# Graph network on one Trainium2 core: one-hots of the second sweep on ScalarE, direction terms of the second tile scaled there and added on VectorE

## The reference, cut to what matters

```
edge_dst, edge_src = src, dst              # of the graph
p0, p1 = pre-layer of x                    # p1: 128 channels x 3 directions
ip1 = sum over m of p1[edge_dst] * p1[edge_src] / 3
w = ssp(edge_attr @ W_f1) @ W_f2 * (ssp([p0, p0, ip1] @ W_s1) @ W_s2)
w1, w2, w3, w4 = split(w, 4)               # 128 each
x0e, x1e = gate-layer of x, at edge_src
out0 = w1 * x0e * sh0 + w4 * (sum over m of x1e[m] * sh1[m]) / sqrt(3)
out1[m] = w2 * x0e * sh1[m] + w3 * x1e[m] * sh0      # m = 1..3
out = segment_sum([out0, out1], edge_dst)
```

## Time and profile before

| | |
|---|---|
| median of 3 runs | 1173.89 us (1171.5 to 1177.24) |
| profiled execution | 1171.3 us, its span 1169.6 us |
| PE busy in the span | 907.8 us (78%) |
| DVE busy | 833.4 us (71%) |
| POOL busy | 731.0 us (63%) |
| ACT busy | 511.1 us (44%) |
| L1135, sums with the one-hot, PE | 184.1 us, x1328 |
| L1137, sums with the scaled one-hots, PE | 134.7 us, x332 |
| L1197, scaled rows, ACT | 161.5 us, x498 |
| L1103, L1106, L1108, dot products, POOL | 122.2, 60.4 and 60.5 us, x83 each |

### The profile page before, as it was taken

One profiled execution on the slowest core, in us unless ns is written; L12 is line 12 of the kernel. 1 busy time (PEld: TensorE's weight loads), 2 busy tenths in 40 slices (PEclk: granted clock), 3 DMA queues, 4 the chain that ended last, 5 costly groups with the idle time before them and its releaser, 6 DMA issues. The chain is left out here.

```text
span 1169.6 us, 23040 instructions
## 1 busy us (share of the span) xinstructions
PE 907.8 (78%) x5587; PEld 623.7 (53%) x5588; DVE 833.4 (71%) x2120; ACT 511.1 (44%) x1484; POOL 731.0 (63%) x768
## 2 busy tenths in 40 slices
PE   1315644449999997675699999999999999999973
PEld 1203322225555553564476777776777776777753
DVE  8441001137777776673599999999999999999967
ACT  1113211012323232463466666666666666666630
POOL 2777777757777773010677777777777777777610
PEclk9998766869999999898799999999999999999997
DMA  9300101157878785012655555555555555555402
GB/s 346 87 15 25 34 24 33 52 162 240 243 240 239 238 240 118 30 65 84 205 171 175 176 168 170 177 165 167 182 164 169 173 171 169 178 164 170 146 4 90
DMA packets 107466, 171.54 MB, mean 147 GB/s; under 512 B 36038, under 2 KB 79162, under 8 KB 107292
## 3 DMA queue, kind: packets, MB, share of 16 engines
q0 software_dynamic: 31584, 122.92, 33.5%
q1 hardware_dynamic: 72060, 46.71, 13.1%
q10 hardware_dynamic: 3776, 1.38, 0.5%
HBM read 151.61 MB, written 19.35 MB: 146 GB/s over the span
## 5 line engine op out<-in xcount | busy, mean ns | idle before, releaser
L749 PE MATMUL ps<-ring,aw 128*128 128x512 f32 x332 | 185.8, 648 | 23.0 <-DVE aw L697 14.3
L1093 POOL DMA_INDIRECT ring<-tab_d,ed x166 | 160.5, 967 | 66.3 <-issue 31.6
L408 POOL DMA_INDIRECT slots_d<-stage,stage_pos x157 | 153.3, 977 | 71.4 <-issue 48.7
L666 POOL DMA_INDIRECT ring<-xt_d,ed x166 | 158.8, 957 | 58.4 <-issue 43.0
L1103 POOL TENSOR_TENSOR dot<-ring,ed 128x768 f32<-128x768 f32 x83 | 122.2, 1472 | 108.7 <-issue 88.3
L1135 PE MATMUL ps<-oh,mm_sb 128*128 128x128 f32 x1328 | 184.1, 282 | 4.9 <-DVE acc L1276 4.9
L1135 PEld LDWEIGHTS ps<-oh,mm_sb 128*128 128x128 f32 x1328 | 161.1, 192 | 23.3 <-issue 17.7
L1197 ACT ACTIVATE ohs<-oh,ed 128x128 f32<-128x128 f32 x498 | 161.5, 389 | 0.0
L1228 ACT ACTIVATE S_sb<-ps 128x512 f32<-128x512 f32 x166 | 90.1, 595 | 115.3 <-PE ps L1184 115.3
L1137 PE MATMUL ps<-ohs,mm_sb 128*128 128x384 f32 x332 | 134.7, 488 | 0.0
L1251 DVE TENSOR_TENSOR ps<-S_sb,ps 128x1024 f32<-128x1024 f32 x83 | 102.0, 1229 | 19.1 <-ACT S_sb L1228 18.3
(11 more groups left out here) (210 smaller groups left out, 1799.9 us busy)
## 6 DMA issues: line engine op xcount, KB each, us to landing
ilb<-f_d SPq DMA_DIRECT2D x83, 128.0 KB
ed<-slots_d SPq DMA_DIRECT2D x166, 38.0 KB, 3.5
tab_d<-tabrow SPq DMA_DIRECT2D x5, 896.0 KB, 3.7
f_d<-ft SPq DMA_DIRECT2D x83, 38.0 KB
slots_d<-fill SPq DMA_DIRECT2D x7, 418.0 KB, 4.4
ring<-xt_d,ed POOLq DMA_INDIRECT x166, 4.0
hcat<-f_d SPq DMA_DIRECT2D x83, 32.0 KB
s0b<-f_d SPq DMA_DIRECT2D x83, 32.0 KB
```

The source lines that it names most:

```text
L408: g.indirect_dma_start(slots_d[:, :], bass.IndirectOffsetOnAxis(ap=stage_pos[:, h, k:k + 1], axis=0), stage[:, h, k, :], None).then_inc(sc ...
L666: gp.indirect_dma_start(xg[:, c, k, :], None, xt_d[:, :], bass.IndirectOffsetOnAxis(ap=ed[:, c, k, JD:JD + 1].bitcast(I32), axis=0))\
L749: pe.matmul(ps[:, 2 * u, :], aw[:, r, k, :], xg[:, c, k, 0:D], start=(alone or k == 0), stop=(alone or k == 1))
L1093: gp.indirect_dma_start(xj[:, r, k, :], None, tab_d[:, :], bass.IndirectOffsetOnAxis(ap=ed[:, c, k, JD:JD + 1].bitcast(I32), axis=0))\
```

## The change

- The one-hots of the second sweep are made on ACT instead of DVE: `away` = |node - row number| by two Abs, then Relu(1 - away) over both tiles. They stand between `inner_out` and the scaled rows.
- `scaled_rows` are made for the group's first tile alone: three instead of six.
- For the second tile ACT scales `w2 * x0e` by each `sh1` into `scaled` (three instructions, behind `log_part`), and DVE adds these to the out1 part of the tile's messages (`add_scaled`, between `accumulate` and `products`). `sums(1)` on PE then needs only the four matmuls with the plain one-hot, and waits for `scaled_added`.
- On POOL `gather` stands ahead of `dots`, and `dots` of group g waits for the turned one-hot of group g+2, which DVE makes in the same round, instead of the one-hot of g-1.
- On ACT `node_part` moves to the end of the round.
- The counters `issue1` and `issue2` become the common `issue`.

```diff
@@ pool
                     gp.wait_ge(xj_in[c], n * 32)
-                    after(gp, oh_ready, g)
+                    gp.wait_ge(ohT_ready, min(g + 3, NG) if isinstance(g, int) else g + 3)
                     after(gp, msg_ready, g - 1)
...
-                pipelined(gp, (2, dots), (0, gather), ring=U)
+                pipelined(gp, (0, gather), (2, dots), ring=U)
@@ tensor, sums(k)
+                        if k == 1:
+                            pe.wait_ge(scaled_added, g + 1)
                         for m in range(4):
-                            pe.matmul(psA[:, P * m:P * m + P], mm_sb[:, u, k, P * m:P * m + P], oh[:, u, k, :],
-                                      start=((alone or k == 0) and m == 0), stop=False)
-                        mm = pe.matmul(psA[:, P:D], mm_sb[:, u, k, D:D + P], ohs[:, u, k, :, :].rearrange("p m n -> p (m n)"),
-                                       start=False, stop=(alone or k == 1))
+                            mm = pe.matmul(psA[:, P * m:P * m + P], mm_sb[:, u, k, P * m:P * m + P], oh[:, u, k, :],
+                                           start=((alone or k == 0) and m == 0), stop=(k == 1 and m == 3))
+                        if k == 0:
+                            mm = pe.matmul(psA[:, P:D], mm_sb[:, u, k, D:D + P], ohs[:, u, :, :].rearrange("p m n -> p (m n)"),
+                                           start=False, stop=alone)
@@ scalar
+                def one_hot(g, c, n):
+                    u = c % 2
+                    act.wait_ge(ed2[c], n * 64)
+                    after(act, sum_ready, upto(g - 2))
+                    for k in range(2):
+                        ins = act.activation(away[:, k, :], iota[:, :], ACT.Abs, scale=-1.0, bias=ed[:, c, k, IL:IL + 1])
+                    ins.then_inc(away_ready, 1)
+                    act.wait_ge(away_ready, g + 1)
+                    act.activation(oh[:, u, :, :], away[:, :, :], ACT.Relu, scale=-1.0, bias=ones[:, 0:1]).then_inc(oh_ready, 1)
...
+                def scaled_messages(g, c, n):
+                    u = c % 2
+                    act.wait_ge(x0_ready, g + 1)
+                    after(act, scaled_added, g)
+                    for m in range(3):
+                        ins = act.activation(scaled[:, m, :], mm_sb[:, u, 1, D:D + P], ACT.Copy, scale=ed[:, c, 1, IL + 2 + m:IL + 3 + m])
+                    ins.then_inc(scaled_ready, 1)
...
-                pipelined(act, (3, factor_out), (2, inner_out), (3, scaled_rows((0, 1), (0, 2))), (1, node_part), (2, log_part),
-                          (3, scaled_rows((0, 3), (1, 1), (1, 2), (1, 3))), ring=U)
+                pipelined(act, (3, factor_out), (2, inner_out), (3, one_hot), (3, scaled_rows((0, 1))), (2, log_part), (3, scaled_messages),
+                          (3, scaled_rows((0, 2), (0, 3))), (1, node_part), ring=U)
@@ vector
+                def add_scaled(g, c, n):
+                    u = c % 2
+                    v.wait_ge(scaled_ready, g + 1)
+                    v.wait_ge(msg_ready, g + 1)
+                    rows = mm_sb[:, u, 1, P:D].rearrange("p (m n) -> p m n", m=3)
+                    v.tensor_tensor(rows, scaled[:, :, :], rows, ALU.add).then_inc(scaled_added, 1)
...
-                def one_hot(g, c, n):
-                    u = c % 2
-                    v.wait_ge(ed2[c], n * 64)
-                    after(v, oh_sh_ready, g - 1)
-                    after(v, sum_ready, upto(g - 2))
-                    for k in range(2):
-                        ins = v.tensor_scalar(oh[:, u, k, :], iota[:, :], ed[:, c, k, IL:IL + 1], None, ALU.is_equal)
-                    ins.then_inc(oh_ready, 1)
...
-                pipelined(v, (2, scaled_features), (3, one_hot), (3, weights), (4, accumulate_first), (3, messages), (2, softplus), (0, turned_one_hot), (4, accumulate),
+                pipelined(v, (2, scaled_features), (3, weights), (4, accumulate_first), (3, messages), (2, softplus), (0, turned_one_hot), (4, accumulate), (3, add_scaled),
                           (1, products), ring=U)
```

More of the change, by code:

```diff
@@ L592, in build @@
         acc_done = sem("acc_done")
-        issue1 = sem("issue1")
         ft_turned = sem("ft_turned")
@@ L661, in gather @@
                         gp.wait_ge(row_done, g - (U - 1))
-                        gp.sem_inc(issue1, 1)
+                        gp.sem_inc(issue, 1)
                     gp.wait_ge(ed_in[c], n * 16)
-                    gp.sem_inc(issue1, 1)
+                    gp.sem_inc(issue, 1)
                     for k in range(2):
@@ L1023, in build @@
         oh = sb("oh", [P, 2, 2, P], scope=sweep2)
-        ohs = sb("ohs", [P, 2, 2, SH - 1, P], scope=sweep2)
+        away = sb("away", [P, 2, P], scope=sweep2)
+        ohs = sb("ohs", [P, 2, SH - 1, P], scope=sweep2)
+        scaled = sb("scaled", [P, SH - 1, P], scope=sweep2)
         ohT = sb("ohT", [P, 2, GE], F32R, scope=sweep2)
@@ L1035, in build @@
         xj_in = [sem(f"xj_in{c}") for c in range(U)]
-        issue2 = sem("issue2")
         oh_ready = sem("oh_ready")
+        away_ready = sem("away_ready")
         ohT_ready = sem("ohT_ready")
@@ L1058, in build @@
         msg_ready = sem("msg_ready")
+        x0_ready = sem("x0_ready")
+        scaled_ready = sem("scaled_ready")
+        scaled_added = sem("scaled_added")
         sum_ready = sem("sum_ready")
@@ L1087, in gather @@
                     gp.wait_ge(ed2[c], n * 64)
-                    gp.sem_inc(issue2, 1)
+                    gp.sem_inc(issue, 1)
                     if not first(g, R):
                         gp.wait_ge(msg_ready, g - (R - 1))
-                        gp.sem_inc(issue2, 1)
+                        gp.sem_inc(issue, 1)
                     for k in range(2):
@@ L1196, in step @@
                         for k, m in which:
-                            ins = act.activation(ohs[:, u, k, m - 1, :], oh[:, u, k, :], ACT.Copy, scale=ed[:, c, k, IL + 1 + m:IL + 2 + m])
-                        if which[-1] == (1, 3):
+                            ins = act.activation(ohs[:, u, m - 1, :], oh[:, u, k, :], ACT.Copy, scale=ed[:, c, k, IL + 1 + m:IL + 2 + m])
+                        if which[-1] == (0, 3):
                             ins.then_inc(oh_sh_ready, 1)
                     return step
+                def scaled_messages(g, c, n):
[5 more added lines that the diff above has]
+                    ins.then_inc(scaled_ready, 1)
                 def inner_out(g, c, n):
@@ L1259, in messages @@
                                     psF.rearrange("p k (s n) -> p k s n", n=P)[:, :, 0:3:2, :],
-                                    xj[:, r, :, 0:P].unsqueeze(2).to_broadcast([P, 2, 2, P]), ALU.mult)
+                                    xj[:, r, :, 0:P].unsqueeze(2).to_broadcast([P, 2, 2, P]), ALU.mult).then_inc(x0_ready, 1)
                     v.wait_ge(dot_ready, g + 1)
```

## The result

The changed kernel takes 1269.66 us (median of 4 runs, 1263.29 to 1274.43), the kernel before 1173.93 us beside it: a ratio of 1.081, interval 1.0748 to 1.0872, 96 us slower. Forecast were 1240 us, 1186 to 1262: the right direction, and 30 us too little. The profiled execution took 1274.43 us, its span 1272.7.

What follows compares the result with a forecast made beforehand. The prediction took the long chain through DVE, PE and ACT to bound the kernel at 6.76 us a round. 80 rounds x 0.82 = 66 us on 1171.3 made 1237, plus 2.6 for the median: 1240 us, range 1186 to 1262.

Steps and rivals of the forecast that it cites:

- Short chain takes over: Second sweep: with the additions alone, the chain through the logarithm binds, so a round can't be under 6.95 us.
- long chain: Chain through DVE, PE and ACT closing in two rounds; said to bind before at 6.77 us, 6.68 after.
- short chain: Chain within one round: products, PE's first sums, hidden layer, ACT's logarithm, DVE up to the products; said to have slack before.
- Hold between L1107 and the addition: POOL's dot products hold DVE's addition until 6.29 us after the products; it ends at 6.71, round 7.58 us.
- 1.1 to 1.3 us: Sign that the forecast is right: DVE's addition lasts this long instead of 0.55 us.
- Second hold, on L1326, just covered: POOL holds this DVE addition until 8.12 us; L1246 could start at 4.11, the logarithm gives 4.16, so no cost.
- forecast wait of 0.1 to 0.5 us for the logarithm: Sign that the forecast is right: DVE waits this long for ACT's logarithm ahead of L1246.
- ACT's one-hots fit ahead of the logarithm: Two Abs and one Relu (0.49 us) fit into ACT's idle time with 0.17 us to spare, without delaying the logarithm.
- Rival 3: Relu isn't in ACT's loaded table; two loads a round cost 205 us, near 1380 us; chance 0.02.
- So I put nothing on the clock: PE will idle about 1.5 us in 7.6 but keeps the full clock, so no cost was counted.
- Rival 1: POOL and DVE don't exclude each other, only the short chain counts: 6.95 us a round, 1189 us; chance 0.20.
- Rival 2: PE's saving carries and the long chain still binds: 6.68 us a round, 1168 us, faster; chance 0.08.

Runs made afterwards that it cites:

- e1: Changed kernel, but POOL's dot products wait for L1326 at the front of the round instead of the turned one-hot: 1216.26 us, ratio 1.0366.
- e5: Changed kernel without DVE's addition; ACT still makes the scaled messages and PE waits for them: 1177.38 us, ratio 1.0028.
- e6: Changed kernel with DVE's addition one round later, right behind L1326, and POOL's dot products behind both: 1180.59 us, ratio 1.0054.
- e2: Changed kernel, but DVE's addition reads its first input from PSUM instead of SBUF; POOL unchanged: 1214.88 us, ratio 1.0343.
- e4: Changed kernel with six unused matmuls of 128 columns on PE ahead of the turning in each round: 1246.65 us, ratio 1.0616.
- e8: Changed kernel with the addition one round later behind L1326, dot products behind both, and DVE's products ahead of the accumulation: 1136.2 us, ratio 0.9674.

## Why the prediction was wrong, step by step

It named the sign, the hold and the length of the round, and left out one term, the clock. It was also wrong about which chain bound before, which the round doesn't show.

- *Short chain takes over*: the direction is right, the picture is not. The prediction gave this chain slack in the kernel before and let the long chain bind. The rows say otherwise. In the traces of before, after, e1, e5 and e6 the median start of the accumulation is 5.16 or 5.17 us after the products, which is 1.03 or 1.04 us after the end of the logarithm (at 4.12), whether the turned one-hot ends at 4.97 (before) or at 4.70 (e5). In the 13 long steady rounds of the changed kernel the logarithm ends at 5.6 to 5.9, and the accumulation again follows 0.95 to 1.16 us later. So DVE's reaching L1246 sooner gains nothing, and before the change the short chain was already the round: 4.12 + 1.03 + 0.60 + 0.95 = 6.70, where 6.72 was measured. With the long chain in charge, e5 would have come to (13.53 - 0.65)/2 = 6.44; it stayed at 6.72, as did e6, which has the addition out of the chain. With the addition in it, the chain grows by the whole 0.47 us: 7.19, as in e1 and e2, not the 6.95 forecast; e1 is 39 and 36 us slower than e5 and e6. What DVE does in that 1.04 us the profile doesn't say ("issue"). In the code the number of the node block is read into a register there, behind the wait for the logarithm; that this is the cause is not shown.
- *Hold between L1107 and the addition*: right: round 7.58 forecast, 7.54 measured. Its share was forecast too large, 0.63 us on top of 6.95, and is 0.35 on top of 7.19; the two errors cancel, since the round hangs on the end of L1107 (6.26 after the products) and not on when DVE comes to the addition. For the same reason the sign "1.1 to 1.3 us" failed: DVE comes to it later, and it lasts 0.90. What the Trainium skill says ("SBUF — State Buffer", "SBUF: two separate sides"), that the other fully blocks, gave 7.71 if taken literally; the trace agrees that the two exclude each other, but the addition ended 0.42 us after L1107 and not 0.55. As a part of the time it is e4 less e1 or e2: 30 to 32 us.
- *Second hold, on L1326, just covered*: right; it lasted 0.64 us in each round and L1273 started at 4.17. The forecast wait of 0.1 to 0.5 us for the logarithm isn't there in the rounds at full clock; the waits of the list above stand in the long rounds.
- *ACT's one-hots fit ahead of the logarithm*: right. Relu took 0.51 us, 0.49 forecast, needed no table load (the sweep has one, at its start, as before), and the logarithm started 0.17 us after its predecessor's end, as forecast. Rival 3 is out.
- *"So I put nothing on the clock"*: this is the step that failed. I read a drain of 20 us at clock 1.00 with PE idle nearly a quarter of the time, and concluded that the idle time of 1.5 us a round would do no harm. PE waits 1.70 us a round ahead of L1124; the clock fell in 17 rounds of the profiled execution, at about 1.65 us each 28 us there, and e4 gives 23 us between the medians. One stretch without a fall isn't evidence for 80 rounds. In e1 and e2, with 1.35 us of waiting in 7.19, the clock fell in one of the steady rounds and in none, beside the first rounds of the sweep.
- The sum then: 1240 + 23 = 1263. The 6 us that remain are in e4 too (1246.65 against 1240). One of them is in the last two rounds, which take 8.78 and 8.37 us where 7.37 and 7.27 stood, 2.5 us against the 1.6 counted; 2.4 are in a single round of 9.97 us at the start of e4's sweep; the rest lies partly outside the rounds: in the two traces e4's first products come 2.0 us later than before (563.9 against 561.9), and 2.5 us more lie behind the start of its last ones. The mean of e4's 68 steady rounds, 7.58 us, is the forecast round.

In steps of medians: before 1174, everything but the addition (e5) +3, the addition out of the chain (e6) +3, in the short chain (e1) +36, held by POOL (e4) +30, the clock +23, which makes 1269.

Rival 1 (no exclusion) is refuted by e1 and e2 from two sides. Rival 2 is refuted by e5: even without the addition the round stayed at 6.72 us, so PE's saving alone doesn't carry. e8 shows where it can: with the accumulation out of the short chain.

## What to carry to other kernels

Before an instruction is added to a full engine, list the chains that close within one round and see on which of them its place lies; the same 0.55 us cost 3 us of the kernel in one place (e6 against e5) and 39 in another (e1 against e5). Idle time ahead of an instruction that is longer where the engine comes earlier shows that the instruction follows another event; count the chain from that event. Then look what POOL does at that moment: a DVE operation with two SBUF inputs (and here also L1293, with one) and a POOL tensor operation run one after the other, as a DVE operation with one input in PSUM did not (0.55 us in e2). And where a change makes PE wait more in each round, its clock is a term of the sum even if the mean share stays high; useless matmuls in the gap show how large it is.

## What the hardware showed that I had not expected

- PE lost its clock in rounds with 1.70 us of waiting in 7.54 us (78.6 us busy in 100), one to nine rounds apart, most often seven, with no wait for the products longer than 2.1 us; each fall cost 1.65 us, as it stretched the part of PE's work that the short chain goes through.
- The hold also reaches POOL's gathers. In e1, whose addition and gather in one round are these rows of the timelines of DVE and POOL, a gather that starts under the addition takes 1.21 us; the mean is 1.11 us there, against 0.97 in the other kernels.

```profile
806.46 0.55 DVE L1304 TENSOR_TENSOR mm_sb<-scaled,mm_sb 128x384 f32<-128x384 f32 x1
```

```profile
806.62 1.21 POOL L1097 DMA_INDIRECT ring<-tab_d,ed  x1 [0.30 <-issue]
```

- The other way round there is no hold. In e6 the addition starts under a running gather, and has its own 0.56 us (76 such rounds, all 0.56). From the timeline of all its engines:

```profile
805.24 0.95 POOL L1097 DMA_INDIRECT ring<-tab_d,ed  x1 [0.30 <-issue]
...
805.90 0.56 DVE L1305 TENSOR_TENSOR mm_sb<-scaled,mm_sb 128x384 f32<-128x384 f32 x1
```

- The operation that comes second has 0.13 us of its own duration behind it when the first one ends: the addition ends 0.42 us after POOL's L1107 in all 80 rounds in which they meet, where its whole duration is 0.55. The prediction had 0.42, from L1301.
- The start of the accumulation follows the end of ACT's logarithm by 1.03 or 1.04 us in the median, with 0.20 us of idle time ahead of it in the kernel before and 0.46 us in the changed one.
